# Graph network on one core: convolutions with a turn between their steps and four banks, score passes with paced look-ups

## What is computed

```python
edge_index = jnp.stack([src, dst])
x = _layernorm(x + _L0_gnn_ref(x, edge_index, edge_attr_64, ...), axis=-1)
x = _layernorm(x + _L1_gnn_ref(x, edge_index, edge_weight, ...), axis=-1)
x = _layernorm(x + _L2_gnn_ref(x, edge_index, ...), axis=-1)
x = _layernorm(x + _L3_gnn_ref(x, src, dst, ...), axis=-1)
```

## Time and profile before

| | |
|---|---|
| median of 3 runs | 5898.77 us (5892.44 to 5901.37) |
| the profiled execution | 5945.03 us, its span 5943.2 us |
| score passes, first to last look-up or store | some 490, 405 and 488 us |
| convolutions 0 to 4 | some 312, 325, 324, 309 and 660 us |
| busy over the span | PE 72%, DVE 65%, ACT 55%, POOL 47% |
| look-ups of the score passes | 588, 0.94 us each |
| look-ups of the convolutions | 980, 0.95 us each |

### The profile page before, as it was taken

How to read it: one execution, slowest core, us unless ns; L and a number is a source line. 1 busy time by engine, 2 the same in 40 slices (tenths; PEclk the granted TensorE clock), 3 DMA queues, 4 the chain that set the end, 5 groups by cost and what they waited for, 6 DMA issues and landing times. The chain is left out here.

```text
span 5943.2 us, 108677 instructions
## 1 busy us (share of the span) xinstructions
PE 4271.4 (72%) x24342; PEld 3042.8 (51%) x24342; DVE 3890.1 (65%) x14954; ACT 3291.7 (55%) x11014; POOL 2792.4 (47%) x2718
## 2 busy tenths in 40 slices
PE   3999995556885996665978885976767676864444
PEld 2667663324663555663546662435555565653333
DVE  5999995445777886777867777983456564433223
ACT  1899994334664775664756675873356563112222
POOL 3888884443431224431224331126556565655565
PEclk9999997778997998887989997998988888986666
DMA  2566664666884776774758874754445454432222
GB/s 66 175 194 196 197 191 168 220 225 217 274 272 155 233 239 208 255 254 146 241 194 271 271 262 153 226 179 121 125 155 166 150 166 130 128 118 67 69 76 62
DMA packets 612939, 1072.27 MB, mean 180 GB/s; under 512 B 107736, under 2 KB 128362, under 8 KB 612764
## 3 DMA queue, kind: packets, MB, share of 16 engines
q1 hardware_dynamic: 537308, 944.74, 47.5%
q0 software_dynamic: 75456, 125.65, 8.7%
HBM read 607.70 MB, written 466.24 MB: 181 GB/s over the span
## 5 line engine op out<-in xcount | busy, mean ns | idle before, releaser
L2385 POOL DMA_INDIRECT got_c<-table,src_row x980 | 927.9, 947 | 622.1 <-issue 254.6
L1387 POOL DMA_INDIRECT src_got_s<-table,src_row x588 | 554.6, 943 | 799.6 <-DVE delta_s L1628 595.6
L1971 POOL TENSOR_TENSOR part_m<-part_m,half_sum_m 128x512 f32<-128x512 f32 x147 | 220.7, 1501 | 916.9 <-DVE half_sum_m L2187 916.9
L1980 PE MATMUL bank<-w_all,dt_m 128*128 128x512 f32 x1176 | 567.9, 599 | 36.3 <-DMA dt_m<-delta_t 34.7
L2509 ACT COPY agg_c<-bank 128x512 f32<-128x512 f32 x245 | 143.4, 585 | 661.9 <-issue 214.0
L1542 ACT ACTIVATE z_s<-z_s,shift_s,dev_s 128x128 f32<-128x128 f32 x1176 | 483.5, 486 | 1.4 <-DVE shift_s L1661 0.9
L2435 PEld LDWEIGHTS bank<-w_c,agg_c 128*128 128x128 f32 x1960 | 327.9, 217 | 262.0 <-issue 261.9
L2435 PE MATMUL bank<-w_c,agg_c 128*128 128x128 f32 x1960 | 357.2, 301 | 99.5 <-issue 97.6
L2433 PE MATMUL bank<-bias_c,first_row 128*128 128x512 f32 x490 | 315.9, 731 | 138.1 <-ACT agg_c L2509 113.5
L790 PEld LDWEIGHTS bank<-w_mean,ht 128*128 128x128 f32 x2352 | 313.3, 194 | 143.6 <-issue 143.6
L2410 PE MATMUL bank<-pick_c,got_c 128*128 128x128 f32 x1960 | 317.1, 314 | 71.2 <-DMA got_c<-table,src_row 59.0
(11 more groups left out here) (326 smaller groups left out, 12028.7 us busy)
## 6 DMA issues: line engine op xcount, KB each, us to landing
table<-rows SPq DMA_DIRECT2D x294, 256.0 KB
x_s<-table SPq DMA_DIRECT2D x294, 256.0 KB
x_c<-table SPq DMA_DIRECT2D x245, 256.0 KB
table<-mid_s SPq DMA_DIRECT2D x196, 256.0 KB
table<-z_s SPq DMA_DIRECT2D x196, 256.0 KB
table<-z_c SPq DMA_DIRECT2D x196, 256.0 KB
own_rows_s<-table SPq DMA_DIRECT2D x147, 256.0 KB
pick_t_s<-picks_t SPq DMA_DIRECT2D x147, 256.0 KB
```

Source lines behind the costliest of these rows:

```text
L1387: nc.gpsimd.indirect_dma_start(out=src_got[r][:, g, :], out_offset=None, in_=tables[l].rows, in_offset=bass.IndirectOffsetOnAxis(ap=src_ro ...
L1971: nc.gpsimd.tensor_tensor(flat(part[r]), flat(part[r]), flat(half_sum[r]), ALU.add).then_inc(parts_added, 1)
L1980: nc.tensor.matmul(b_h[k % n_h][:, :], dt[b.slot][:, k, :], w_all[:, l, :, :].rearrange("p h d -> p (h d)"), start=True, stop=True).then_i ...
L2385: nc.gpsimd.indirect_dma_start(out=got[r][:, g, :], out_offset=None, in_=t_in.rows, in_offset=bass.IndirectOffsetOnAxis(ap=src_row[:, t:t ...
```

## The change

Score passes: each of the four look-ups of a batch has a wait of its own, on four events of one turn (`pace`). Convolutions: the sums get four banks in the gcn layers (0 to 2) where they had two, `sum_edges` comes first in PE's turn, own rows one turn later, the product and what follows another turn later. The fifth convolution keeps its order.

```diff
@@ edge_scores, block.gpsimd @@
+                        def pace(b, g):
+                            if g == 0:
+                                pool.wait_ge(delta_made, b - 3)
+                            elif first:
+                                if g == 1:
+                                    pool.wait_ge(turned, 2 * b - 4)
+                                elif g == 2:
+                                    pool.wait_ge(h_made, 2 * b - 5)
+                                else:
+                                    pool.wait_ge(y_made, 2 * b - 5)
+                            elif g == 1:
+                                pool.wait_ge(y_made, 2 * b - 5)
+                            elif g == 2:
+                                pool.wait_ge(turned, 2 * b - 3)
+                            else:
+                                pool.wait_ge(y_made, 2 * b - 4)
...
-                            if b > 3:
-                                pool.wait_ge(delta_made, b - 3)
                             for g in range(GB):
                                 t = b * GB + g
+                                if b > 3:
+                                    pace(b, g)
@@ convolve @@
-                b_sum, b_own, b_y = bank[0:2], bank[2:4], bank[4:6]
+                b_sum, b_own, b_y = bank[0:2] * 2 if sage else bank[0:4], bank[2:4], bank[4:6]
...
-                            b = at(6 if norm else 4)
+                            b = at(7 if norm else 5)
                             if b and not placing:
                                 store(b)
...
-                            hold(pe, agg_made, b.count(1, -1))
+                            hold(pe, agg_made, b.count(1, -1 if sage else -3))
...
                         def step_gcn_norm(at):
+                            b = at(1)
+                            if b:
+                                sum_edges(b)
                             b = at(2)
                             if b:
                                 add_own(b)
-                            b = at(1)
-                            if b:
-                                sum_edges(b)
-                            b = at(2)
+                            b = at(3)
                             if b:
                                 product(b)
...
                         def step_sage_relu(at):
                             b = at(1)
                             if b:
-                                add_own(b)
                                 sum_edges(b)
-                            b = at(2)
+                                add_own(b)
+                            b = at(3)
                             if b:
                                 product(b)
```

More of the change, by code:

```diff
@@ L2366, in step @@
                                 load_residual(b)
-                            b = at(6 if norm else 4)
+                            b = at(7 if norm else 5)
                             if b and not placing:
                                 store(b)
-                        skewed(sp, nb, 6 if norm else 4, step, 4)
+                        skewed(sp, nb, 7 if norm else 5, step, 4)
                         if not placing:
@@ L2407, in sum_edges @@
                             pe.wait_ge(pick_made, b.count(1, 1))
-                            hold(pe, agg_made, b.count(1, -1))
+                            hold(pe, agg_made, b.count(1, -1 if sage else -3))
                             for k in range(GB):
-                                ins = nc.tensor.matmul(b_sum[r][:, k * P:(k + 1) * P], got[b.slot][:, k, :], pick[r][:, k, :],
+                                ins = nc.tensor.matmul(b_sum[b.slot][:, k * P:(k + 1) * P], got[b.slot][:, k, :], pick[r][:, k, :],
                                                        start=k == 0, stop=sage, skip_group_check=True)
@@ L2424, in add_own @@
                                 for k in range(GB):
-                                    ins = nc.tensor.matmul(b_sum[r][:, k * P:(k + 1) * P], x[b.slot][:, k, :], own[r][:, k, :],
+                                    ins = nc.tensor.matmul(b_sum[b.slot][:, k * P:(k + 1) * P], x[b.slot][:, k, :], own[r][:, k, :],
                                                            start=False, stop=True, skip_group_check=True)
@@ L2483, in _ @@
                         if sage:
-                            skewed(pe, nb, 3 if norm else 2, step_sage_norm if norm else step_sage_relu, 4)
+                            skewed(pe, nb, 3, step_sage_norm if norm else step_sage_relu, 4)
                         else:
-                            skewed(pe, nb, 2, step_gcn_norm if norm else step_gcn_relu, 4)
+                            skewed(pe, nb, 3, step_gcn_norm if norm else step_gcn_relu, 4)
                     @block.scalar
@@ L2508, in sums_out @@
                                 act.wait_ge(carry_added, b.count(1, 1))
-                            nc.scalar.copy(flat(agg[r]), b_sum[r][:, :]).then_inc(agg_made, 1)
+                            nc.scalar.copy(flat(agg[r]), b_sum[b.slot][:, :]).then_inc(agg_made, 1)
                         def deviation(b):
@@ L2524, in step_relu @@
                         def step_relu(at):
+                            b = at(2)
+                            if b:
+                                sums_out(b)
                             b = at(0)
@@ L2527, in step_relu @@
                                 diagonals(b)
-                            b = at(2 if sage else 1)
-                            if b:
-                                sums_out(b)
                         def step_gcn_norm(at):
-                            b = at(4)
+                            b = at(5)
                             if b:
@@ L2541, in step_gcn_norm @@
                                 diagonals(b)
-                            b = at(3)
+                            b = at(4)
                             if b:
@@ L2556, in _ @@
                         if norm:
-                            skewed(act, nb, 4, step_sage_norm if sage else step_gcn_norm, 4)
+                            skewed(act, nb, 4 if sage else 5, step_sage_norm if sage else step_gcn_norm, 4)
                         else:
-                            skewed(act, nb, 2 if sage else 1, step_relu, 4)
+                            skewed(act, nb, 2, step_relu, 4)
                     @block.vector
@@ L2612, in carry_over @@
                             dve.wait_ge(summed, b.count(1, 1))
-                            carry(dve, b, (scanned, spread, carry_added), tails, now[b.half], carried, b_sum[b.half], dve_pace)
+                            carry(dve, b, (scanned, spread, carry_added), tails, now[b.half], carried, b_sum[b.slot], dve_pace)
                         def step_relu(at):
@@ L2655, in _ @@
                         if norm:
-                            skewed(dve, nb, 4 if sage else 3, step_sage_norm if sage else step_gcn_norm, 4)
+                            skewed(dve, nb, 4, step_sage_norm if sage else step_gcn_norm, 4)
                         else:
-                            skewed(dve, nb, 2, step_relu, 4)
+                            skewed(dve, nb, 3, step_relu, 4)
         t = tables + [final]
```

2 lines of the change are left out of this document (removed).

## The result

The changed kernel takes 5752.53 us (median of 4 runs, 5743.35 to 5761.14), the kernel before 5898.58 us in the same comparison: ratio 0.9754, interval 0.9733 to 0.9774, 146 us less. The forecast was 5763 us. The sum came out within 11 us, but that is luck, for its terms did not: the score passes gave 197 us where the forecast had 116, and the convolutions took 29 us or more where it had them give 20.

What follows compares the result with a forecast made beforehand. No engine bounds the whole; PE's news is held while POOL's look-ups follow each other. First and third pass -80, second pass -36, convolutions -20 sum to -136: 5898.77 to 5763 us, range 5625 to 5890.

Steps and rivals of the forecast that it cites:

- PE's news is held while look-ups follow each other: Score passes and convolutions: news of finished PE work arrives together about 1.1 us behind POOL's run of look-ups.
- The rival by which PE is truly late: Score passes: PE really ends late under DMA's load, pauses on POOL change nothing, time stays 5899 us; chance 0.13.
- First and third pass: Score passes one and three: waits bring a batch to 8.7 us, -80 us together, bounds 0 and -127.
- What ends a batch then? DMA.: First and third score pass: 8.17 us of transfers at a highest share of 0.94 allow hardly under 8.7 us a batch.
- the first rival: Everything is won: DMA at its full, score passes at 8.17 and 6.4 us a batch, -197 us, kernel 5682; chance 0.20.
- second rival: Cited where PE, not DMA, would end a score-pass batch; the rival listed second says news is not held, 5899 us, 0.13.
- Second pass: Second score pass: waits bring a batch from 8.01 to 7.2 us, -36 us, bounds 0 to -70.
- The pacing is the same: Second score pass: waits act as in the other passes, but events come less evenly, so two thirds of the way to 6.8.
- Convolutions: New order and banks: 6.0 us a batch for 6.21 in convolutions 1 and 2, -17; 0 and 3 together -3; sum -20.
- POOL is freed for two batches at a time more often: Convolutions: more runs of eight look-ups with one longer pause, 6.03 us a batch instead of 6.14.
- only the dependent rest of the last batch, which is as long as before: Ends of four convolutions: the added turn costs nothing; were it a full turn of 4.7 us, +19.
- The third rival: Convolutions: longer runs of look-ups hold more, +172 us there, kernel 5955; sign: pauses over 5 us; chance 0.12.

Runs made afterwards that it cites:

- e3: Kernel before plus a 128x512 POOL memset behind each score-pass look-up: 5626.7 us for 5902.8 (first kind of chip), ratio 1.0021 on the second kind.
- e8: Changed kernel, memsets replacing score-pass waits, convolution 1 in old order with four banks, memsets in convolutions 0, 2, 3, 4: ratio 1.0034 first kind, 1.0109 second.
- e6: Changed kernel with later events in the second score pass and one more wait in all convolutions: 5643.3 us, ratio 0.9564 to the kernel before, first kind.
- e1: Kernel before plus only the waits between score-pass look-ups: 5134.2 us for 5134.8, ratio 0.9992, second kind of chip.
- e2: Changed kernel with score passes as before, so the convolutions' change alone: 5146.3 us for 5134.8, ratio 1.0018; again 5145.0, ratio 1.0023; both second kind.
- e9: Kernel before plus 128x512 memsets behind score-pass look-ups and one wait in all convolutions, old order: 5147.6 us for 5133.9, ratio 1.0030, second kind.

## Why the prediction held in sum, and where its terms failed

**The bound (held).** The reading that PE's news is held while look-ups follow each other is what e3 and e8 show: a break of 0.70 us and nothing else takes DVE's 1.9 us a batch away, one of 0.31 leaves it. The rival by which PE is truly late and only the model hides it is out. As to the Trainium skill, "Perfetto Trace Analysis", section "Tensor Engine Instruction (MATMUL, LD_WEIGHTS)", by which the end is computed, the runs show that it was near the truth here: where nothing is held, ACT starts 0.04 us after the modelled end.

**First and third pass: -80 forecast, -191 measured.** The failed step is "What ends a batch then? DMA.", with the 8.17 us of transfers that were worked out from a share of 0.85. A share that no stretch had passed is no ceiling: after, it is 0.99 over 50 us. Nor was the 8.17 a need, though it bounded the term at -127: the same transfers now go in 7.5 us a batch. DMA's share of busy time in a stretch that waits for something else doesn't say how fast it can go. The second error is PE's 8.0 us a batch, taken from windows at a granted clock of 0.92; without the idle time the clock is 1.00, the 128x512 matmul of `hidden` goes from 0.654 to 0.594 us, and a batch needs 7.4 (0.986 of 7.5). That is where the pass now ends: 7.5 us a batch, PE at 49.29 of 50. It is nearly what the first rival said against itself, "PE would have to be busy 98% of the time". The stretch from 1500 to 1550 us moved 359 GB/s, where 348 had been the most over 20 us. By the ceiling of 435 GB/s in the Trainium skill, "DMA: Bandwidth & Descriptors", section "Where 436 GB/s comes from", PE would be the bound, and the trace agrees in that PE is full; that more than 359 GB/s can be had, no run shows, since DMA's share stands at 1.01 there. (Where the prediction speaks at this point of its "second rival", its first, in which everything is won, is meant.)

**Second pass: -36 forecast, -5 measured.** The failed step is "The pacing is the same". The counts of its waits were never held against the state in which POOL reaches them. e6 gives 41 us with later events and e3 73 with breaks.

**Convolutions: -20 forecast, +29 by the two profiled executions.** The convolutions of e3, which are those of before, take 1880.3 us, 23 less than in the profiled execution of before, so that the cost may be as much as some 52; the least that the prediction gave was 0. Two steps failed. One is "POOL is freed for two batches at a time more often": it was in convolution 0 (15 runs of eight for 9, and 5 to 11 us less), but hardly in 1 and 2, of which 17 us were expected (7 for 6 and 6 for 4), and there the pauses behind runs of four grew, from 1.58 to 2.10 us on average in convolution 1. The sums do stand free of own rows, but own rows and product now stand ahead of the next sums behind each hold, and with norm they hang on ACT's deviation and DVE's scale. The other is the turn more at the end, "only the dependent rest of the last batch, which is as long as before": it costs 15 us, near the 19 that were named and not counted. The third rival had the direction right, and its sign, pauses grown over 5 us, came up. But it named another mechanism, longer runs, and there were none of sixteen; e8 shows that the four banks cost nothing.

**The sum.** By the profiles, -197 in the passes and +29 in the convolutions make -168 of the 184 between the two spans. Another 11 us lie ahead of the first pass and 5 between and behind the stages, where nothing was changed: the profiled execution of before took longer than its others. It stood 46 us above its median and that of after 9, and the medians differ by 146. So the first and third pass gave 111 us more than forecast, the second pass and the convolutions 31 and 49 less, which leaves 31 more; the profiled executions overstate the difference by 38, of which 16 lie in what wasn't changed, and that takes 22 away. What is left is 9 of the 10 us between 136 and 146. Errors of this size that cancel are luck; of the mechanisms, that of the hold was right.

## What to carry to other kernels

When results of one engine are taken up in bursts that end a fixed time behind another engine's run of indirect DMAs, put a break into that run before rebuilding anything: it is one line, and says at once whether the hold is the cause. Here 0.70 us was long enough and 0.33 was not, and it paid only where the engine had time to spare. A wait meant as a break must be on something that hasn't come yet when it is reached; read that from the trace, by counting, for each stage that uses it. And don't take an engine's need per item, or a resource's ceiling, from a stretch in which it was kept waiting: both the clock and the share rose when the wait went. A turn more of depth is paid at the end of every stage: look at the gap between stages too, not only at the pace inside them.

## What was not expected of the hardware

The hold is there on some chips and not on others, with the same code and the same durations of instructions. The kernel before takes 764 us more on the first kind (5899 for 5135). That all of it is the hold is not shown: between the profiled executions of before and e1, 811 us apart, 293 us lie in the passes and 396 in the convolutions, but 121 ahead of the first pass, where nothing was tried. What differs between the chips isn't settled.

Where the hold is there, it was seen with look-ups 0.30 to 0.33 us apart and not with 0.70. In the first pass before (1400 to 1818 us), of the results of PE that DVE or ACT waited for, 13 of 43 that ended during a run's second look-up were taken up within 0.1 us, and none of 67 from the third on; on a chip of the second kind it was all 39 from the third on (e2, 1290 to 1590 us). In convolution 1, 8 of 23 that ended during the third still came through. The news comes 1.1 us or a little more behind a run of four, and 1.8 to 2.1 us behind a run of eight. DVE's and ACT's news isn't late: in convolution 1 before, all 60 starts in which one of them waited for the other from a run's third look-up on came within 0.04 us.

The breaks and waits that gain 2 to 5% on a chip of the first kind cost next to nothing on the others: nothing in e1, 0.2% in e3, 0.3% in e9. With memsets in all convolutions too, it was 1.5%.
